# An attention and feed-forward layer with its loops written out, its weight words scanned in 88 pieces, and the exponentials' two waits in the other order

## The reference

```python
q = rope(x @ Wq.T + bq); k = rope(x @ Wk.T + bk); v = x @ Wv.T + bv   # 16 heads of 16
scores = softmax(q @ k.T / sqrt(256)); out = (scores @ v) @ Wo.T
x = layernorm(x + out)
h = silu(x @ w1.T * s1) * (x @ w2.T * s2)        # 1024 wide
h = gelu(h @ h1.T * t1); h = gelu(h @ h2.T * t2)
x = layernorm(x + h @ w3.T * s3)
```

## Time and profile before

| what | value |
| --- | --- |
| median of 3 runs | 3755.98 us (3754.24 to 3756.96) |
| profiled execution | 3752.6 us, its span 3751.0 us |
| PE busy | 3478.5 us (93%) |
| DVE busy | 2933.2 us (78%) |
| ACT busy | 2455.1 us (65%) |
| granted TensorE clock, mean of the span | 0.967 |

### The profile page before, as it was taken

One profiled execution on the slowest core, in us unless ns is written; L12 is line 12 of the kernel. 1 busy time (PEld: TensorE's weight loads), 2 busy tenths in 40 slices (PEclk: granted clock), 3 DMA queues, 4 the chain that ended last, 5 costly groups with the idle time before them and its releaser, 6 DMA issues. The chain is left out here.

```text
span 3751.0 us, 63608 instructions
## 1 busy us (share of the span) xinstructions
PE 3478.5 (93%) x20194; PEld 1507.5 (40%) x20194; DVE 2933.2 (78%) x3148; ACT 2455.1 (65%) x4472; POOL 196.4 (5%) x352
## 2 busy tenths in 40 slices
PE   8569999999999999999999999999999789999999
PEld 4223333233323323332332333233332278888887
DVE  6598999899989989998998899899988045555554
ACT  2108888788878878887888888788888712222222
POOL 3200000000000000000000000000000011111100
PEclk9759999999999999999999999999999989999999
DMA  8940000000000000000000000000000141111100
GB/s 210 216 142 12 12 12 12 13 12 12 12 13 23 12 13 12 12 12 13 12 12 13 16 20 12 13 12 12 12 8 8 35 157 35 40 47 36 35 18 12
DMA packets 64535, 125.92 MB, mean 34 GB/s; under 512 B 12551, under 2 KB 24904, under 8 KB 63032
## 3 DMA queue, kind: packets, MB, share of 16 engines
q1 hardware_dynamic: 59528, 114.02, 10.8%
q0 software_dynamic: 4704, 7.81, 0.7%
HBM read 90.59 MB, written 41.16 MB: 35 GB/s over the span
## 5 line engine op out<-in xcount | busy, mean ns | idle before, releaser
L678 DVE TENSOR_REDUCE group_max<-wide 128x2 f32<-128x1024 f32 x2048 | 2406.2, 1219 | 280.9 <-PE wide L509 280.7
L656 ACT ACTIVATE probs<-scores 128x512 f32<-128x512 f32 x4046 | 2200.2, 599 | 464.0 <-PE scores L602 369.7
L602 PE MATMUL scores<-q_sb,k_all 51*128 51x512 f32 x3968 | 999.8, 500 | 126.2 <-ACT probs L656 40.0
L534 PE MATMUL sums<-probs,v_all 128*17 128x512 f32 x8192 | 1088.7, 604 | 1.3 <-ACT probs L656 0.9
L602 PEld LDWEIGHTS scores<-q_sb,k_all 51*128 51x128 f32 x3968 | 371.9, 184 | 1292.5 <-ACT probs L656 1265.5
L509 PE MATMUL wide<-k_all,q_sb 48*128 48x512 f32 x4096 | 805.5, 457 | 75.5 <-DVE group_max L678 50.8
L509 PEld LDWEIGHTS wide<-k_all,q_sb 48*128 48x128 f32 x4096 | 395.9, 190 | 393.7 <-DVE group_max L678 364.0
L1061 ACT ACTIVATE whole_hid<-acc,scale 128x512 f32<-128x512 f32 x128 | 84.6, 687 | 349.3 <-PE acc L942 344.6
L942 PE MATMUL acc<-hid_a,h1T 128*128 128x512 f32 x1024 | 240.4, 395 | 2.0 <-DVE hid_a L1153 2.0
L942 PE MATMUL acc<-hid_b,h2T 128*128 128x512 f32 x1024 | 241.5, 396 | 0.0
L534 PEld LDWEIGHTS sums<-probs,v_all 128*17 128x17 f32 x8192 | 135.9, 95 | 255.2 <-ACT probs L656 166.6
(11 more groups left out here) (84 smaller groups left out, 1239.3 us busy)
## 6 DMA issues: line engine op xcount, KB each, us to landing
k_all<-k_parts SPq DMA_DIRECT2D x96, 128.0 KB, 5.0
q_sb<-q_parts SPq DMA_DIRECT2D x192, 64.0 KB, 2.3
w_words<-ff_weights SPq DMA_DIRECT2D x32, 352.0 KB, 3.1
q_parts<-parts SPq DMA_DIRECT2D x16, 512.0 KB, 5.4
k_parts<-parts SPq DMA_DIRECT2D x16, 512.0 KB, 6.2
heads<-mixed SPq DMA_DIRECT2D x32, 256.0 KB, 2.5
heads_sb<-heads SPq DMA_DIRECT2D x8, 1024.0 KB, 4.8
shares<-shares_dram POOLq DMA_DIRECT2D x112, 64.0 KB, 2.2
```

The source lines that it names most:

```text
L534: last = pe.matmul(sums[32 * j:32 * j + HD + 1, :], v_all[:, g, kt, j], probs[(kt * HG + j) % RING][:], start=(kt == 0), stop=(kt == KT - 1))
L602: pe.matmul(scores[(s + e) % BANKS][:], k_all[rows, g * GP + j, kt * P:(kt + 1) * P], q_sb[g][rows, j], start=True, stop=True).then_inc(sc ...
L656: act.activation(probs[n % RING][:], bank, ACT.Exp, scale=INV_SCALE)\
L678: dve.reduce_max(group_max[:, n], wide[n % 2][:], AX_X).then_inc(wide_free, 1)
```

## The change

1. The loops over `c` in `attend` and over `half` in `feed_forward` are written out on TensorE, ScalarE, VectorE, SP and GpSimd.
2. GpSimd's queue loads the weight words from the five inputs themselves, in 88 pieces of 128 x 256 words, into three buffers in turn. VectorE scans a piece behind the maximum reduction n = 12, 32 and 52 of a unit, two or three a unit. The copies to `w_dram` stay on SP, one in each of the chunks 1 to 5, behind the load of the queries.
3. In the exponential, ScalarE's code waits for `scored` first and for `probs_free` second.
4. In `attend`'s TensorE code a new `unit` is defined whose step makes two scores, then one and one, with a maximum group behind each of the first two heads. The former `unit` stands below it in the file, under the same name.

```diff
+PIECE = 256
+PIECES = [(name, n) for name, (rows, cols) in W_SHAPES.items() for n in range(rows * cols // (P * PIECE))]
...
-            for name, (at, rows, cols) in W_AT.items():
-                sp.dma_start(w_dram[at:at + rows * cols].rearrange("(r c) -> r c", c=cols), io[name]).then_inc(w_copied, 16)
-            sp.wait_ge(w_copied, 16 * len(W_AT))
...
-            load_words(0)
+
             place_shift(0, 0)
-            with sp.Fori(0, NCH - 1) as c:
+            for c in range(NCH - 1):
                 for g in range(NG):
-                    load_words(c * NG + g + 1)
                     place_shift(c * NG + g + 1, (g + 1) % NG)
                     finish(c, g)
                     load_q(c + 1, g)
+                    if 0 < c <= len(W_AT) and g == 0:
+                        name, (at, rows, cols) = list(W_AT.items())[c - 1]
+                        sp.dma_start(w_dram[at:at + rows * cols].rearrange("(r c) -> r c", c=cols), io[name]).then_inc(w_copied, 16)
...
+            def load_words(u):
+
+                for i in pieces_beside(u):
+                    name, n = PIECES[i]
+                    if i >= WORDS:
+
+                        pool.wait_ge(scanned, i - WORDS + 2)
+                    words = io[name].rearrange("r c -> (r c)").rearrange("(n p w) -> n p w", p=P, w=PIECE)[n]
+                    pool.dma_start(w_words[i % WORDS][:], words).then_inc(words_in[i % WORDS], 16)
...
+            load_words(0)
+            load_words(1)
             pool.wait_ge(exps_done, BANKS)
             split_shift(0)
-            with pool.Fori(1, UNITS) as u:
+            load_words(2)
+            for u in range(1, UNITS):
 
                 pool.wait_ge(exps_done, (u - 1) * SLOTS + TURN_AT + 1 + BANKS)
                 split_shift(u)
+                if u + 2 < UNITS:
+                    load_words(u + 2)
...
+                    for j in range(HG):
+                        n = kt * HG + j
...
+                        if j != 1:
+
+                            pe.wait_ge(exps_done, u * SLOTS + s + (PAIR if j == 0 else 1))
...
+                        if 0 < j < HG - 1 and groups:
+                            max_group(*groups[j - 1])
...
-            with pe.Fori(0, NCH - 1) as c:
+            for c in range(NCH - 1):
...
                     s = slot(n, not last)
+                    act.wait_ge(scored, u * SLOTS + s + 1)
                     if n % HG == 0:
 
                         act.wait_ge(probs_free, u * KT + n // HG + 1)
-                    act.wait_ge(scored, u * SLOTS + s + 1)
...
                     dve.reduce_max(group_max[:, n], wide[n % 2][:], AX_X).then_inc(wide_free, 1)
+                    if n % 20 == 12 and n // 20 < len(pieces_beside(u)):
+                        scan(pieces_beside(u)[n // 20])
...
-                with pe.Fori(0, NCH // 2 - 1) as half:
+                for half in range(NCH // 2 - 1):
```

More of the change, by code:

```diff
@@ L387, in attend @@
         w_copied = sem("w_copied")
-        words_in = sem("words_in")
+        words_in = [sem(f"words_in{p}") for p in range(WORDS)]
         scanned = sem("scanned")
@@ L457, in _ @@
                 sp.wait_ge(mixed_free[p], 16 + 16 * UNITS // 2)
+            sp.wait_ge(w_copied, 16 * len(W_AT))
         @block.gpsimd
@@ L586, in unit, with after, groups_beside @@
                     groups = groups_beside(c, g, kt, left)
+                    for j in range(HG):
+                        n = kt * HG + j
+                        if n == TURN_AT and left > 0:
+                            pe.wait_ge(exps_done, u * SLOTS + n + 1)
+                            max_turn(u + 1, n % BANKS, scored)
+                        s = slot(n, left > 0)
+                        if j != 1:
+                            pe.wait_ge(exps_done, u * SLOTS + s + (PAIR if j == 0 else 1))
+                        rows = slice(j % PAIR * HALF, j % PAIR * HALF + SLOT)
+                        pe.matmul(scores[s % BANKS][:], k_all[rows, g * GP + j // PAIR, kt * P:(kt + 1) * P],
+                                  q_sb[g][rows, j // PAIR], start=True, stop=True).then_inc(scored, 1)
+                        if 0 < j < HG - 1 and groups:
+                            max_group(*groups[j - 1])
+                    if kt > 0:
+                        sum_over(u, g, kt - 1, False)
+                    else:
+                        sum_over(u - 1, g - 1, KT - 1)
+            def after(c, g):
+                return c + (g + 1) // NG, (g + 1) % NG
+            def groups_beside(c, g, kt, left):
+                steps = 1 + (kt + LEAD) // KT
+                if steps > left:
+                    return []
+                for _ in range(steps):
+                    c, g = after(c, g)
+                kt = (kt + LEAD) % KT
+                return [(c, g, n) for n in range(kt * GROUPS, (kt + 1) * GROUPS)]
+            def unit(c, g, first=False, left=2):
+                u = c * NG + g
+                pe.wait_ge(shift_in, u * 96 + 192)
+                for kt in range(KT):
+                    groups = groups_beside(c, g, kt, left)
                     for j in range(GP):
@@ L661, in _ @@
             unit(0, 0, first=True)
-            with act.Fori(0, NCH - 1) as c:
+            for c in range(NCH - 1):
                 for g in range(1, NG):
@@ L671, in _, with scan @@
         def _(dve):
+            def scan(i):
+                dve.wait_ge(words_in[i % WORDS], 16 * (i // WORDS) + 16)
+                dve.wait_ge(scanned, i + 1)
+                dve.scalar_tensor_tensor(out=bits[:], in0=w_words[i % WORDS][:].bitcast(I32), scalar=LOW_BITS, in1=bits[:],
+                                         op0=ALU.bitwise_and, op1=ALU.bitwise_or).then_inc(scanned, 1)
             def maxima(u):
-                if not (isinstance(u, int) and u == 0):
+                if u > 0:
                     dve.wait_ge(top_ready, u)
@@ L704, in _ @@
             dve.memset(sums[:], 0.0).then_inc(sums_free, 1)
-            scan(0)
-            maxima(1)
-            scan(1)
-            with dve.Fori(2, UNITS) as u:
+            for u in range(1, UNITS):
                 maxima(u)
-                scan(u)
-            dve.wait_ge(scanned, UNITS + 1)
+            dve.wait_ge(scanned, len(PIECES) + 1)
             dve.reduce_max(low_bits[:], bits[:], AX_X).then_inc(scanned, 1)
-            dve.wait_ge(scanned, UNITS + 2)
+            dve.wait_ge(scanned, len(PIECES) + 2)
 def feed_forward(nc, io, heads_dram, shares_dram, w_dram, low_bits, out):
@@ L1080, in _ @@
             gates(0)
-            with act.Fori(0, NCH // 2 - 1) as half:
+            for half in range(NCH // 2 - 1):
                 for p in range(2):
@@ L1221, in _ @@
             invert(1)
-            with dve.Fori(0, NCH // 2 - 1) as half:
+            for half in range(NCH // 2 - 1):
                 for p in range(2):
```

25 lines of the change are left out of this document (8 added, 17 removed).

## The result

| | changed kernel | kernel before |
| --- | --- | --- |
| median | 3697.85 us of 4 runs (3696.09 to 3701.14) | 3755.11 us of 4 runs on the same chip (3751.8 to 3756.96) |
| profiled execution | 3699.49 us, span 3697.8 | 3752.6 us, span 3751.0 |
| granted TensorE clock, mean | 0.972 | 0.967 |
| instruction packets | 159, 2.61 MB | 196, 3.21 MB |

The ratio is 0.9849, with a 95% interval of 0.9832 to 0.9867: faster, by 57 us.

A forecast was written before the change was run, and what follows sets the result against it. It took a ring of PE and ScalarE, 2.60 us a step, as the bound; 3752.6 - 5.7 - 31 - 13.3 + 4.8 + 0.7 - 5.5 - 2.3 = 3700.3 us, plus 3.4 for the median: 3703, range 3688 to 3732.

The forecast's parts named there:

- The ring of PE and ScalarE: In a step of `attend`, PE and ScalarE each wait for the other; this sets the step at 2.60 us.
- The exponentials' waits: Written-out ScalarE code: the event takes `probs_free`, every step 2.60 us; units 0, 29 and 30 gain 5.7 us.
- Rival (a): ScalarE's exponentials: the event keeps the late wait despite the swap, giving 3762 us; chance 0.09.
- The scores' order: TensorE's step in `attend`: matmul order stays as before, the new `unit` being shadowed by the old; 0 us.
- The turnings: Loop branches in `attend`: six stops of PE for its instructions and a lower clock behind them go; 31 us gained.
- the scan at the turn: Step 27 of a unit: without the scan on VectorE the second pair goes 0.46 us earlier; 13.3 us in 29 units.
- The pieces: 88 scans on VectorE, 0.33 us each, nearly covered by PE's idle time: 0.055 a piece, 4.8 us added.
- The start: Ahead of unit 0, VectorE no longer waits for its first words and scan: 5.5 us gained.
- The queues: SP's copies and GpSimd's loads of pieces delay no shift: 0 us.
- (b): Straight instruction stream in `attend` not fetched in time, PE standing still for each packet: 3851 us; chance 0.02.
- (c): Words come late from GpSimd's queue and VectorE stops 88 times: 4122 us; chance 0.02.
- The net's loop: In `feed_forward`, two loop turnings go, with steps otherwise 90.0 us: 2.3 us gained.

The follow-up runs named there:

- the announced order: Changed kernel with the former `unit` deleted, so that the new one's order of TensorE takes effect: 3696.74 us, ratio 0.9849.
- waits back: Changed kernel with ScalarE's code waiting for `probs_free` first and `scored` second again: 3757.0 us, ratio 1.0014.
- sums early: Changed kernel with TensorE's `sums` ahead of the second pair of scores and both maximum groups behind it: 3758.1 us, ratio 1.0017.

## Why the prediction was right, point by point

**What bounds the kernel.** Right. The ring of PE and ScalarE sets the step at 2.60 us; the announced order leaves it, a later wait of 0.06 lengthens it by as much (waits back, sums early), 59 and 60 us a run.

**The exponentials' waits.** Right, with their price. In written-out code the event takes the wait that is written second, as the trace's event rows show. The 5.7 us for units 0, 29 and 30 came: the step is 2.60 in all three, up to where the clock falls in unit 30. Rival (a), 3762 with the event keeping the late wait, came out at 3757.0 where its condition was made true by hand. What I had not seen is that the rule turns around in a loop; the prediction did not need it, but the expectation for the kernel before with swapped waits failed by 63 us on it.

**The scores' order.** Right at 0, since the order did not take effect; where it does, it is worth 2.3 us.

**The turnings, and the scan at the turn.** The mechanism of both was right and their sum too. Of the 31 + 13.3 us predicted, 31 + 28 x 0.46 = 43.9 fell to units 1 to 28; these gained 46.2. Some 1.6 of the difference is in the turnings: units 1 to 28 took 2388.8 us before, which is 32.6 above 28 x 84.15, so the upper end of the forecast's own bracket was the better figure. In step 27 the second pair follows the first by 1.67 us, where 2.14 was and 1.7 was due:

```profile
925.48 0.19 PEld L655 LDWEIGHTS scores<-q_sb,k_all 51*128 51x128 f32 x2 [0.85 <-ACT probs L709]
...
926.01 1.08 ACT L709 ACTIVATE probs<-scores 128x512 f32<-128x512 f32 x2 [0.32 <-PE scores L655]
926.18 0.19 PEld L521 LDWEIGHTS wide<-k_all,q_sb 48*128 48x128 f32 x2 [0.41 <-DVE group_max L738]
...
927.15 0.19 PEld L655 LDWEIGHTS scores<-q_sb,k_all 51*128 51x128 f32 x2 [0.45 <-ACT probs L709]
```

The 0.46 us a unit were booked to the scan alone. Of these the scan has 0.35 and the writing out some 0.12: the total holds, the split does not. Writing out also shortens the step of the turn itself, a term that I had at nothing.

**The pieces.** Mis-sized: 4.8 us predicted, 0 measured. I let two pairs directly behind each other cost 0.055, a figure that no row gave; the pair behind a piece comes on time to 0.01. The 0.33 us of hold is exact. The other bound, cover failing, was nearer than it looked: at 0.79 us it fails, by 0.34 to 0.44 a piece.

**The start.** The term was nearly right, and its effect on the run did not come. From VectorE's first reduction to its first of `maxima(1)` it is 255.04 - 181.06 = 73.98 us; before, the same stretch was 256.38 - 177.41 = 78.97. That is 5.0 less, against the 4.8 that the start and the two early pieces make. Of the 5.0, the words have 4.2: in the two kernels with the loops written out and the words unmoved the stretch was already 78.2. The changed kernel's rows:

```profile
181.06 14.80 DVE L738 TENSOR_REDUCE group_max<-wide 128x2 f32<-128x1024 f32 x13 [5.86 <-PE wide L521]
195.78 0.41 DVE L729 SCALAR_TENSOR_TENSOR bits<-w_words,bits 128x256 int32<-128x256 int32 x1
...
255.04 5.68 DVE L738 TENSOR_REDUCE group_max<-wide 128x2 f32<-128x1024 f32 x5
```

But the stretch began 3.65 us later (181.06, not 177.41), so unit 0 starts only 1.5 earlier. Of that, 2.8 us are in `project`, whose code is the same and whose end scatters from 171.6 to 175.5 us over the profiles of all kernels. The other 0.9 us lies between the issue of the first queries and the first reduction: 5.7 to 5.8 us in the four profiles with the words on SP's queue, 6.2 to 6.8 in the eight with the words on GpSimd's. The rows of the query loads show where. These are the fourth to sixth, first of before, then of the changed kernel, from issue to landing (shortest, median, longest):

```profile
DMA to landing us min/median/max: 2.4/2.4/2.6
DMA to landing us min/median/max: 2.4/3.4/3.5
```

GpSimd issues its first words between the fourth and the fifth of these loads. The first four land as before, the fifth and the sixth 0.9 to 1.0 us later, and TensorE's first matmul follows the sixth by 0.05 to 0.06 us in both kernels. I had priced the words' new queue at 0 and looked only at the shifts.

**The queues.** No shift is late and VectorE never stands idle ahead of line 729: rivals (b) and (c) have no row for them. PE has no "issue" wait at scores from 600 to 2650 us; written out, the program even has fewer instruction packets, 159 instead of 196.

**The net's loop.** Right: 2.4 us against 2.3. The steps are 90.0 us now in all windows, also where a turning lay:

```profile
L992 PE MATMUL acc<-hid_a,h1T x145: 394/394/397, 2991.3 to 3085.0; 128*128 128x512 f32 x145
L992 PE MATMUL acc<-hid_a,h1T x166: 394/394/397, 3081.3 to 3179.9; 128*128 128x512 f32 x166
L992 PE MATMUL acc<-hid_a,h1T x166: 394/394/397, 3171.2 to 3269.9; 128*128 128x512 f32 x166
```

**What was left out.** "A granted clock of 1.00 from unit 1 on" was wrong for the last two units of `attend`: the fall at the end of unit 30 costs 3.7 us (two steps of 3.87 and 4.05 us and one of 3.39 where 2.60, 2.60 and 2.40 are usual). The last of these is the first step of unit 31, so the table's +0.9 is in the 3.7. Together with the start's lost 3.3 that is 7.0 us. The other way go the 4.8 of the pieces that were not spent and the 2.3 that units 1 to 28 gained beyond their terms, 7.1 us. So part of the close agreement, 3697.8 against a sum of 3698.7 on the span's scale, is errors of both signs. The 5 us between the forecast of 3703 and the median have another source: I added 3.4 for a median above the profiled time, as before, and here the median (3697.85) lies 1.6 below it (3699.49).

## What to carry to other kernels

Where an engine's instruction waits for two semaphores, find out in the order which of the two stays on the instruction, and see that it is the one that comes last: in code written out that was the wait written first, in a loop the wait written last, and either mistake cost some 60 us of 3755 here (0.06 us, some 900 to 1000 times). An edit that turns a loop into straight code or back must be judged together with this; the loops alone made the kernel slower and with the two lines faster. An engine in a ring with another pays for whatever makes the ring longer and for nothing else: work hides beside it only as far as its idle time reaches, here 0.33 us without a trace and 0.79 us with a loss of about 0.4.

## What was not expected of the hardware

- A semaphore wait that moves from an exponential to an instruction just ahead of it lengthens the way from its release to the exponential from 0.33 to 0.39 us in written-out code and to 0.41 in a loop with a register instruction.
- TensorE's granted clock fell to the lower level for 3 to 17 us at the end of unit 30 in seven of ten profiles. In the window ahead, without maximum groups, PE is busy 3.23 of 4.60 us; in unit 8, where the clock is 1.00, 80.02 of 83.60:

```profile
939.50:1023.10 83.60, 80.02 (x515) 25.78 (x513) 76.36 (x68) 70.02 (x130) 3.54 (x8) 1.00 0.05 14
2855.00:2859.60 4.60, 3.23 (x24) 0.88 (x16) 0.00 (x0) 3.84 (x8) 0.00 (x0) 0.99 0.04 9
```

- Why the same kernel's fall lasted 10 us in one profile and 14 in the other, and why before's profile has none, stays open.
- The first word loads on GpSimd's queue make the query loads that SP issues behind them land 0.4 to 1.1 us later: the sixth takes 2.55 to 2.65 us to landing in four profiles without them, 3.04 to 3.65 in eight with them. By what they hold each other up stays open; no kernel tried the words on a third queue.
